# A convolution's kernel table split once and stored in two parts, its Toeplitz rows loaded per part

## What is computed

```python
x = x + _L0_cond_ref(x, log_dt, C, log_A_real, A_imag, D, length)   # a long convolution in time
x = x + einsum('bct,bcd->bdt', x, W1[itok])                         # a 32x32 mix chosen per batch item
x = x + einsum('bct,bcd->bdt', x, W2[itok])                         # another
x = x + lora_mlp(x, W_gate, W_up, W_down, A_*, B_*, itok2)          # gated MLP 512-1376-512 with LoRA
# the convolution:
K = 2.0 * einsum('hn,hnl->hl', Ct, exp(P)).real      # one kernel of 512 taps per channel h
y = causal_convolution(u, K) + u * D[:, None]
return y * (arange(T) < length)                      # masked by each item's length
```

## Time and profile before

| | us |
|---|---|
| three runs | 1174.17, 1175.84, 1176.66; median 1175.84 |
| profiled execution | 1175.31, of which the profile's span is 1173.5 |
| preparation | 0 to 40.3 |
| convolution, to the landing of its last store | 40.3 to 128.8 |
| first inputs of the tiles, until PE works again | 128.8 to 142.3 |
| tile 0 and part of tile 1 | 142.3 to 186.7 |
| steady tiles | 186.7 to 1130.6 |

### The profile page before, as it was taken

The page is one execution under the profiler, slowest core; times in us unless marked ns, Lnnn a source line. Parts: engine busy times, 40 slices in busy tenths (PEclk is TensorE's granted clock), DMA queues, the critical chain, the costliest instruction groups (busy, mean ns, idle before and its releaser), DMA issues.

```text
span 1173.5 us, 19301 instructions
## 1 busy us (share of the span) xinstructions
PE 1062.2 (91%) x6176; PEld 932.3 (79%) x6176; DVE 294.4 (25%) x550; ACT 441.4 (38%) x691; POOL 526.4 (45%) x334
## 2 busy tenths in 40 slices
PE   3577369999999999999999999999999999999998
PEld 3576258888887878888888888787878888888886
DVE  7566212221221222121211222221212221212221
ACT  7543234243333334343424333333433333433331
POOL 0587364343434444443534443444445353544431
PEclk9799679999999999999999999999999999999999
DMA  8688323333324233332333333323333233333321
GB/s 327 221 288 281 121 82 99 102 112 91 108 72 123 69 110 105 98 111 81 109 106 107 89 108 93 114 64 113 93 105 110 81 112 97 107 94 115 96 68 36
DMA packets 100922, 135.52 MB, mean 115 GB/s; under 512 B 26340, under 2 KB 59365, under 8 KB 100901
## 3 DMA queue, kind: packets, MB, share of 16 engines
q1 hardware_dynamic: 99380, 133.35, 37.4%
q10 hardware_dynamic: 1520, 1.92, 0.6%
HBM read 118.21 MB, written 16.99 MB: 115 GB/s over the span
## 4 chain that ended last, share of the span: by engine, by line
SPq 35%; PE 22%; issue 12%; POOL 11%; DMA 11%; ACT 7%; DVE 3%; ACTq 0%; DVEq 0%; POOLq 0%
SPq L339 14%; DMA braw<-in_tb 10%; POOL bst L443 9%; PE ps L979 8%; SPq L188 7%; PE ps L948 6%; ACT bst L572 5%; PE ps L1021 5%; SPq L267 4%; SPq L347 3%; SPq L322 2%; SPq L329 2%; PE ps L969 1%; PE ps L1010 1%; SPq L315 1%
## 5 line engine op out<-in xcount | busy, mean ns | idle before, releaser
L443 POOL TENSOR_TENSOR bst<-braw,bst 128x1024 fp32r<-128x1024 f32 (+1 forms) x96 | 212.2, 2211 | 246.7 <-ACT bst L572 246.7
L979 PE MATMUL ps<-wg_hi,x_hi 128*128 128x512 f32 (+2 forms) x768 | 298.0, 388 | 1.7 <-DVE x_lo L832 1.7
L979 PE MATMUL ps<-wg_hi,x_lo 128*128 128x512 f32 (+2 forms) x768 | 292.1, 380 | 0.0
L979 PE MATMUL ps<-wg_lo,x_hi 128*128 128x512 f32 (+2 forms) x768 | 291.9, 380 | 0.0
L424 POOL TENSOR_TENSOR x_raw<-x_raw,xb 128x512 f32<-128x512 f32 x32 | 41.2, 1286 | 322.2 <-DMA xb<-in_x 322.2
L572 ACT ACTIVATE bst<-braw,odd 128x1024 fp32r<-128x1024 f32 (+1 forms) x96 | 103.6, 1079 | 184.8 <-DMA braw<-in_tb 184.1
L979 PEld LDWEIGHTS ps<-wg_hi,x_lo 128*128 128x128 f32 x768 | 145.2, 189 | 25.7
L979 PEld LDWEIGHTS ps<-wg_hi,x_hi 128*128 128x128 f32 x768 | 145.8, 190 | 22.9 <-issue 2.0
L979 PEld LDWEIGHTS ps<-wg_lo,x_hi 128*128 128x128 f32 x768 | 145.8, 190 | 20.6
L1021 PE MATMUL ps<-wd_hi,at_hi 128*128 128x288 f32 (+1 forms) x704 | 159.0, 307 | 1.8 <-DVE at_lo L855 1.4
L588 ACT ACTIVATE at_hi<-ps 128x512 fp32r<-128x512 f32 (+1 forms) x96 | 54.0, 562 | 274.0 <-PE ps L1010 273.1
(11 more groups left out here) (142 smaller groups left out, 1309.0 us busy)
## 6 DMA issues: line engine op xcount, KB each, us to landing
braw<-in_tb SPq DMA_DIRECT2D x256, 128.0 KB, 2.7
braw<-in_tb SPq DMA_DIRECT2D x128, 96.0 KB, 2.4
adraw<-in_tad SPq DMA_DIRECT2D x128, 88.0 KB, 2.1
ur<-in_xT SPq DMA_DIRECT2D x16, 512.0 KB, 4.3
x1p<-yo SPq DMA_DIRECT2D x16, 512.0 KB, 3.3
x_raw<-x1p SPq DMA_DIRECT2D x32, 256.0 KB, 2.8
xb<-in_x SPq DMA_DIRECT2D x32, 256.0 KB, 3.0
agraw<-in_ta SPq DMA_DIRECT2D x128, 64.0 KB, 2.3
```

Of the source, the lines that this page charges most:

```text
L443: sub(v, b_from(q), v.bitcast(F32), ALU.subtract).then_inc(s["blo"], 1)
L979: last = mm(bank[:, 0:n], x3s[a][:, k, :], wgs[b][:, k, o:o + n], start=(k == 0 and a + b == 0), stop=False, skip_group_check=True)
```

## The change

The table `kf` is split while it is still 16 x 1024: ACT copies it to `kf_hi`, DVE subtracts to `kf_lo`. Both are stored, to `kpad[0]` and `kpad[1]`, the second after the first. The Toeplitz matrix of a pair is now two DMAs of 512 KB, one from each part, straight into the float32r tile `tp`, which holds three pairs (`NTP = 3`). `ts_hi` and `ts_lo` are gone. SP issues the first three pairs as soon as both parts are in DRAM, then pair q + 3 when PE is done with pair q. The input `ur` keeps its two pairs, the output `yo` too. The loops are written out. The eight `w_low` of POOL now stand at the head of its program.

```diff
-    kpad = nc.dram_tensor("kpad", (C, P + T), F32, kind="Internal").ap()
+    kpad = nc.dram_tensor("kpad", (2, C, P + T), F32, kind="Internal").ap()
...
+        def load_toeplitz(eng, q):
+            for a in range(2):
+                src = kpad[a, 2 * q:2 * q + 2, 0:T]
+                src = bass.AP(src.tensor, src.offset, [[1, P], [P + T, 2], [1, T]])
+                eng.dma_start(tp[:, q % NTP, a].bitcast(F32), src).then_inc(s[f"tt{q % NTP}"], 16)
+
+        def load_u(eng, q):
+            p = q % 2
+            eng.dma_start(ur[:, 2 * p:2 * p + 2, :], xT[2 * q:2 * q + 2].rearrange("c p w -> p c w")
+                          ).then_inc(s[f"u{p}"], 16)
...
+            sp.wait_ge(s["kout"], 64)
+            for q in range(NTP):
+                load_toeplitz(sp, q)
+
+            for q in range(C // 2):
+                if q + 2 < C // 2:
+                    sp.wait_ge(s["usp"], 2 * q + 2)
+                    load_u(sp, q + 2)
+                if q + NTP < C // 2:
+                    sp.wait_ge(s["y"], 2 * q + 2)
+                    load_toeplitz(sp, q + NTP)
+                sp.wait_ge(s["ev"], 2 * q + 2)
+                sp.dma_start(x1p_bct[:, 2 * q:2 * q + 2, :], yo[:, q % 2]).then_inc(s[f"yst{q % 2}"], 16)
...
-            def lows(it):
-                for k in range(4):
-                    pool.wait_ge(s["thi"], it * 4 + k + 1)
-                    nc.gpsimd.tensor_tensor(ts_[1][:, k, :], tr[:, k, :], ts_[0][:, k, :].bitcast(F32),
-                                            ALU.subtract).then_inc(s[f"tsp{k}"], 1)
-
-            for it in range(C // 4):
-                lows(it)
-                if it < 6:
-                    w_low(it)
-            for k in range(4):
-                pool.wait_ge(s[f"tsp{k}"], C // 4)
+            for n in (0, 1, 2, 3, 4, 5, 9, 10):
+                w_low(n)
...
             ag_low(0)
-            w_low(9)
-            w_low(10)
             b_low(0, 0, 0)
...
             act.wait_ge(s["kf"], 1)
-            act.dma_start(kpad[:, P - 1:P - 1 + T].rearrange("h (i j) -> i h j", j=UI), kf[:]).then_inc(s["kout"], 16)
-
-            for k in range(4):
-                act.wait_ge(s[f"u{k // 2}"], 16)
-                nc.scalar.activation(us[0][:, k, :], ur[:, k, :], ACT.Copy).then_inc(s["uhi"], 1)
-            w_high((7,))
-            act.wait_ge(s["kout"], 32)
+            nc.scalar.activation(kfs[0][:], kf[:], ACT.Copy).then_inc(s["khi"], 1)
+            act.wait_ge(s["khi"], 1)
+            act.dma_start(kpad[0, :, P - 1:P - 1 + T].rearrange("h (i j) -> i h j", j=UI), kfs[0][:].bitcast(F32)
+                          ).then_inc(s["kout"], 16)
+            act.wait_ge(s["klo"], 1)
+            act.dma_start(kpad[1, :, P - 1:P - 1 + T].rearrange("h (i j) -> i h j", j=UI), kfs[1][:].bitcast(F32)
+                          ).then_inc(s["kout"], 16)
+            act.wait_ge(s["kout"], 64)
             act.wait_ge(s["tst"], 16)
...
+            def u_high(h):
+                q = h // 2
+                act.wait_ge(s[f"u{q % 2}"], 16 * (q // 2) + 16)
+                if h >= 4:
+                    act.wait_ge(s["y"], h - 3)
+                nc.scalar.activation(us[0][:, h % 4, :], ur[:, h % 4, :], ACT.Copy).then_inc(s["uhi"], 1)
+
+            for h in range(4):
+                u_high(h)
             act.dma_start(w_part(wg_raw, wd_raw, NW - 1), w_hbm(NW - 1)).then_inc(s[f"wl{NW - 1}"], 16)
-
-            w_high(range(8, NW - 1))
-
-            highs(0, True)
+            w_high(range(7, NW - 1))
+            for h in range(4, 8):
+                u_high(h)
             w_high((NW - 1,))
-            with act.Fori(1, C // 4) as it:
+            for h in range(8, C):
+                u_high(h)
+            act.wait_ge(s["y"], C)
...
+            dve.wait_ge(s["khi"], 1)
+            dve.wait_ge(s["kf"], 1)
+            V.tensor_tensor(kfs[1][:], kf[:], kfs[0][:].bitcast(F32), ALU.subtract).then_inc(s["klo"], 1)
+
             w_low(6)
...
+            def out_of_psum(h):
+                q = h // 2
+                dve.wait_ge(s["y"], h + 1)
+                if q >= 2:
+                    dve.wait_ge(s[f"yst{q % 2}"], 16 * (q // 2))
+                V.tensor_tensor(yo[:, q % 2, h % 2, :], yp[h % 4], mk[:], ALU.mult).then_inc(s["ev"], 1)
+
+            for h in range(4):
+                u_low(h)
+            w_low(7)
+            w_low(8)
+            for h in range(C):
+                out_of_psum(h)
+                if h + 4 < C:
+                    u_low(h + 4)
...
+            for h in range(C):
+                q = h // 2
+                pe.wait_ge(s["usp"], h + 1)
+                pe.wait_ge(s[f"tt{q % NTP}"], 32 * (q // NTP) + 32)
+                if h >= 4:
+                    pe.wait_ge(s["ev"], h - 3)
...
-            pe.wait_ge(s["wlo"], 6)
+            pe.wait_ge(s["wlo"], 8)
```

More of the change, by code:

```diff
@@ L59 @@
 K_PN = 568
+NTP = 3
 UCOLS, VCOLS = C * UN, C * UI
@@ L126, in cond_resid_kernel @@
         zer = sb("zer", [C, P])
-        kf = sb("kf", [UN, C, UI])
+        kf_hi = sb("kf_hi", [UN, C, UI], F32R)
+        with ExitStack() as raw_only:
+            kf = sbin(raw_only)("kf", [UN, C, UI])
+        kfs = [kf_hi, sb("kf_lo", [UN, C, UI], F32R)]
         wms = sb("wms", [C, NCOND, 2, C])
@@ L133, in cond_resid_kernel @@
         us = [sb("us_hi", [P, 4, KT * B], F32R), sb("us_lo", [P, 4, KT * B], F32R)]
-        ts_ = [sb("ts_hi", [P, 4, T], F32R), sb("ts_lo", [P, 4, T], F32R)]
-        yo = sb("yo", [P, 4, T])
-        tr = sb("tr", [P, 4, T])
+        tp = sb("tp", [P, NTP, 2, 2, T], F32R)
+        yo = sb("yo", [P, 2, 2, T])
         ur = sb("ur", [P, 4, KT * B])
@@ L161, in cond_resid_kernel @@
         outb = sb("outb", [P, T])
-        names = """pk cst cstp small lens w12 zer kf kout wm wms tst u0 u1 tt0 tt1
-            a1 da dch ph tg kuv kps uhi thi usp0 usp1 usp2 usp3 tsp0 tsp1 tsp2 tsp3 whi wlo wlv y0 y1 y2 y3
-            ev0 ev1 ev2 ev3 yst0 yst1 done wz msk
+        names = """pk cst cstp small lens w12 zer kf kout wm wms tst u0 u1 tt0 tt1 tt2
+            a1 da dch ph tg kuv kps uhi usp khi klo whi wlo wlv y
+            ev yst0 yst1 done wz msk
             xin xsum x1hi x1lo wbd x3mm x3n x3t x3hi x3lo
@@ L249, in _ @@
             sp.dma_start(ixs[:], idx).then_inc(s["small"], 16)
-            for p in range(2):
-                sp.dma_start(ur[:, 2 * p:2 * p + 2, :], xT[2 * p:2 * p + 2].rearrange("c p w -> p c w")
-                             ).then_inc(s[f"u{p}"], 16)
+            for q in range(2):
+                load_u(sp, q)
             for n in range(NW - 1):
@@ L487, in _ @@
             act.wait_ge(s["zer"], 1)
-            act.dma_start(kpad[:, 0:P - 1], zer[:, 0:P - 1]).then_inc(s["kout"], 16)
+            for a in range(2):
+                act.dma_start(kpad[a, :, 0:P - 1], zer[:, 0:P - 1]).then_inc(s["kout"], 16)
             act.wait_ge(s["da"], 1)
@@ L518, in _ @@
-            act.dma_start(w_part(wg_raw, wd_raw, NW - 1), w_hbm(NW - 1)).then_inc(s[f"wl{NW - 1}"], 16)
-            w_high(range(8, NW - 1))
[L522 to L529, removed]
@@ L780, in _ @@
             V.tensor_tensor(d0, d0, dsk[:], ALU.add).then_inc(s["kf"], 1)
+            dve.wait_ge(s["khi"], 1)
+            dve.wait_ge(s["kf"], 1)
+            V.tensor_tensor(kfs[1][:], kf[:], kfs[0][:].bitcast(F32), ALU.subtract).then_inc(s["klo"], 1)
             w_low(6)
[L784 to L817, removed]
+            def u_low(h):
+                dve.wait_ge(s["uhi"], h + 1)
+                V.tensor_tensor(us[1][:, h % 4, :], ur[:, h % 4, :], us[0][:, h % 4, :].bitcast(F32),
+                                ALU.subtract).then_inc(s["usp"], 1)
+            def out_of_psum(h):
[4 more added lines that the diff above has]
+                V.tensor_tensor(yo[:, q % 2, h % 2, :], yp[h % 4], mk[:], ALU.mult).then_inc(s["ev"], 1)
@@ L938, in _ @@
             PASSES = ((0, 0), (0, 1), (1, 0))
-            def conv_block(it, first):
-                for k in range(4):
-                    pe.wait_ge(s[f"usp{k}"], it + 1)
-                    pe.wait_ge(s[f"tsp{k}"], it + 1)
-                    if not first:
-                        pe.wait_ge(s[f"ev{k}"], it)
-                    for c in range(KT):
-                        for a, b in PASSES:
-                            last = mm(yp[k][:, c * P:T], us[a][:, k, c * P:(c + 1) * P], ts_[b][:, k, 0:T - c * P],
-                                      start=(c == 0 and a + b == 0), stop=(c == KT - 1 and a == 1))
-                    last.then_inc(s[f"y{k}"], 1)
-            conv_block(0, True)
-            with pe.Fori(1, C // 4) as it:
-                conv_block(it, False)
+            for h in range(C):
[4 more added lines that the diff above has]
+                    pe.wait_ge(s["ev"], h - 3)
+                for c in range(KT):
+                    for a, b in PASSES:
+                        last = mm(yp[h % 4][:, c * P:T], us[a][:, h % 4, c * P:(c + 1) * P],
```

(3 more changed lines are left out.)

11 lines of the change are left out of this document (2 added, 9 removed).

## The result

| | before | after |
|---|---|---|
| median (range), us | 1175.26 (1174.17 to 1176.66) | 1211.43 (1210.75 to 1214.1) |
| profiled execution, span | 1173.5 | 1210.2 |
| `kf` complete; its store (before) or its copy to `kf_hi` (after) starts | 29.7 | 46.9 |
| first Toeplitz issue | 32.68 | 52.58 |
| last store of the convolution landed | 128.77 | 169.20 |

The ratio is 1.0305, interval [1.0283, 1.0327]: the change makes the kernel slower by 36.2 us. The forecast was 1205.2 with a range of 1185 to 1220. The span grew by 36.7: 17.2 before `kf`, 2.7 for the split, 20.5 in the convolution, -3.7 behind it.

The account below looks back on a forecast made before the run. The convolution was taken as bound by loads, partly their bytes and partly the round trip from freed slot to next landing. Terms 18.7 + 2.6 + 15.3 - 7.2 = +29.4 us gave 1205.2 us, range 1185 to 1220.

Parts of the forecast that it names:

- The forecast's case: All four terms together, +29.4 us, giving a median of 1205.2 us; chance 0.55.
- Part 1: Preparation: six POOL weight subtractions each cost DVE's chain to kf one POOL instruction, +18.7 us; bounds 0, 6.2 and 18.8.
- The rival in which DVE keeps its turn: Preparation: only two of the six subtractions hold DVE up, 12.5 us less, 1192.7 us; chance 0.14.
- Part 2: Between kf and the second store: an ACT copy and a DVE subtraction with two hand-offs, +2.6 us.
- Part 3: Convolution, first Toeplitz issue to last store's landing: 111.4 us against 96.1, +15.3; bounds +9.2 and +20.5.
- so I take the middle, 6.7 us a pair: Convolution: pace chosen between the DMA bytes' 6.23 and the ur loop's 7.1 us a pair.
- its 7.1: Convolution: loop of ur landing (median 4.3), us_hi, us_lo, evacuation, hand-offs and store issue, 7.1 us a pair.
- Two of the signs named for this part: Convolution: ur issues 6.2 to 7.1 us apart, and DMA share above 0.9.
- The other floor: Convolution: DMA time for two Toeplitz loads, one ur and one store, 6.23 us a pair against PE's 3.95.
- The price of 1.77: Convolution: DMA time of one 512 KB Toeplitz load, 1.77 us of all 16 engines, against 1.42 for an ur.
- The rival of cheap Toeplitz rows: Convolution: Toeplitz rows cost no more than ur rows once the queue never runs dry, 11.2 us less, 1194.0; chance 0.08.
- Part 4: Tile 0: without w_low(9) and w_low(10), b_low starts 6.3 us earlier and PE need not restart at 1.2 GHz, -7.2 us.

Follow-up runs that it names:

- alone in the kernel before: Kernel before, with POOL's w_low(0) to w_low(5) moved to the head of its program: 1191.51 us, ratio 1.013.
- alone in the gap: Kernel before, with only w_low(9) and w_low(10) moved from tile 0 to between the convolution's end and the first tile's inputs: 1168.07 us, ratio 0.9939.
- changed order: Changed kernel, with DVE evacuating both heads of a pair before the two us_lo of two pairs on: 1193.47 us, ratio 1.0151.
- POOL held back: Changed kernel, with POOL starting its weight subtractions only when DVE has made kf_lo: 1202.82 us, ratio 1.0235.
- one Toeplitz load, old order: Changed kernel, loading only the high part of the Toeplitz rows, one 512 KB load a pair instead of two: 1204.54 us, ratio 1.025.
- rows 256 bytes apart: Changed kernel with both evacuations before the us_lo, Toeplitz row starts 256 bytes apart instead of 4, both loads reading one part of kpad: 1186.9 us.
- the same row: Changed kernel with both evacuations before the us_lo, Toeplitz loads reading one row, starting on 256 bytes, for all 128 partitions: 1196.47 us.
- 260 bytes apart: Changed kernel with both evacuations before the us_lo, Toeplitz row starts 260 bytes apart, both loads reading one part of kpad: 1189.32 us.
- the same row, 4 bytes on: Changed kernel with both evacuations before the us_lo, one Toeplitz row for all 128 partitions, starting 4 bytes off 256 bytes: 1196.25 us.
- paced: Changed kernel, with both evacuations before the us_lo and POOL's eight subtractions let go one a pair after six us_lo: 1177.89 us, ratio 1.0018.
- moved into the convolution: Kernel before, with only w_low(9) and w_low(10) moved from tile 0 into the fifth and sixth round of the convolution: 1174.66 us, ratio 0.9985.

## Why the prediction was right, point by point

The time lay inside the range, 6.2 above the forecast. The forecast's case came true and not a rival; its terms, measured in the profiled executions:

| term | predicted | measured | shown by |
|---|---|---|---|
| 1. POOL against DVE's chain | +18.7 | +17.2 | trace; alone in the kernel before, +17.1 to the store of `kf` |
| 2. the split | +2.6 | +2.7 | trace |
| 3. the convolution | +15.3 | +20.5 | trace; order, bytes and both apart |
| 4. tile 0 | -7.2 | -3.7 | trace; alone in the gap, -6.9 behind the convolution |

**Part 1** was right in mechanism and count: six turns. The price was taken as the whole POOL instruction, 3.13; DVE's own instruction runs inside what is left, so the excess was about 2.8. The rival in which DVE keeps its turn fell: DVE's rows at 23.40 to 35.58 follow each other without a gap, and each waits once. The rule of the Trainium skill (SBUF — State Buffer, "SBUF: two separate sides") that the loser waits out the whole instruction agrees with the rows of 3.00 to 3.14 us. That L727 and L728, with one tensor input of 32 elements, wait too agrees with the same page ("Who interferes with whom"), which lets `tensor_scalar` enter the modes that take the pair.

**Part 2** held: 46.90 to 52.58 is 5.7 against 3.0.

**Part 3** had the two floors and went wrong in the choice between them; the weak step is "so I take the middle, 6.7 us a pair". The loop ran at 7.27, above its 7.1. The reason given for the middle, that the median landing of 4.3 holds waits behind other transfers, took off what was not there to take: the loop's landings were 4.87 on the mean, and with a quarter of the traffic gone still 4.53, with the pair at 6.93. The bytes came in only through these 0.34 us. The floor by bytes, 5.77 when the queue is full, lay below and was no reason to go down from the loop's number. In numbers: the first stretch was 1.3 shorter than predicted (14.0 to the landing of the third `ur`), the 13 pairs took 93.8 instead of 87.1, the end 8.8 instead of 8.95. Two of the signs named for this part did not come: the pairs lie outside 6.2 to 7.1, and the DMA share stayed under 0.9.

That 7.1 itself came so near is partly luck: the landings were 0.57 longer than the median it took, the steps between them 2.40 instead of 2.8. And that the stage's +20.5 is the very number of the upper bound is chance: longer pairs and a shorter start cancel.

The other floor was over-read for a full queue: predicted 6.23 a pair, measured 5.77. The price of 1.77 for a Toeplitz load was no misreading of its window, though. It comes back in the stage after the change: 0.89 x 7.27 less 0.67 x 6.93, with and without the load (shares of the windows of 80 to 110 us), is 1.83 us of all 16 engines, an estimate. In the changed order the same difference is 1.04 x 5.77 less 0.98 x 4.67, or 1.42, and the pair itself is 1.10 shorter, which is a lower bound if the loop holds part of the 4.67. So the busy time that a load takes was no fixed price here; in the fuller queue it was smaller. The rival of cheap Toeplitz rows was right that they cost less than 1.77 once the queue is full; that they cost no more than `ur` rows is not shown. It had little effect, because the bytes do not set this kernel's pace: half of the Toeplitz loads left out gave 6.9 us, not the 25 to 29 of a kernel that waits for bytes.

The rule of the Trainium skill named there (DMA: Bandwidth & Descriptors, "How a descriptor splits into AXI transactions") is not shown to be the reason. By that rule the 71 beats are the charge for some starts only; over starts 4 bytes apart it is 65 to 72 and 68 on the mean. An estimate by it for rows moved off 256 bytes is 32 x 1.42 x 4.4 / 64, or 3 us. The runs with spread rows are 2.4 us apart in the median with intervals wider than that, and their pairs take 5.30 off 256 bytes and 5.35 on it: they can neither confirm nor exclude it, but most of the 6.6 us must come from something else. The two kernels with one row for all do not test it, since it charges a start 4 bytes on only one beat more.

**Part 4** was right in its mechanism and too high by 3.5 in the profiled execution. `b_low` started when predicted. Two later landings took part of it: `xb` landed after 3.05 instead of 2.73, `agraw` after 3.85 instead of 2.20. And PE idled 2.2 us instead of 8, but its clock fell all the same: it started again at 2.4 GHz (a matmul of 512 columns took 0.39 at 202.56), and from 203.06 on each took 0.63. Two windows (PE's busy time first, its granted clock third from the end):

```profile
199.50:202.00 2.50, 0.30 (x3) 0.06 (x1) 0.52 (x1) 1.80 (x3) 2.50 (x3) 1.00 0.11 20
202.00:207.00 5.00, 5.00 (x17) 4.01 (x18) 0.56 (x1) 1.96 (x3) 0.27 (x2) 0.66 0.34 100
```

The twelve matmuls took 4.34 against 4.69 before, so most of the 1.9 for the clock did not come. But how much of this is the kernel and how much the one execution? The rest of the span was 1044.7 and 1045.6 in the two kernels with `w_low(9)` and `w_low(10)` in tile 0. In the kernels that have them elsewhere it was:

| kernel | rest, us |
|---|---|
| after | 1041.0 |
| POOL held back | 1039.0 |
| DVE's order | 1038.2 |
| one Toeplitz load, old order / changed order | 1039.3 / 1040.6 |
| rows 256 bytes apart / the same row | 1037.4 / 1039.6 |
| 260 bytes apart / the same row, 4 bytes on | 1038.8 / 1040.0 |
| paced | 1037.7 |
| before, moved into the convolution / into the gap | 1039.2 / 1037.8 |

The gain is 3.7 to 7.3 us against 1044.7, with a mean near 6; after's own execution has the least of it. The estimate of 7.2 was at the upper edge, and some 2 of the 3.5 that the table misses belong to after's one execution.

The two errors, 5.2 too little in part 3 and 3.5 too much in part 4, point the same way, and 1.5 too much in part 1 against them; that the whole came within 6.2 owes a little to this.

## What to carry to other kernels

Moving idle-looking POOL work forward is not free when it reads SBUF beside a DVE chain on the critical path: count one POOL instruction for each DVE instruction it meets, and put it where DVE waits for something else anyway (the gap at 128.8 us was worth 7 us, the same two instructions in the convolution nothing). In a loop with few buffers write out what each engine does in order before costing its transfers: one subtraction standing in front of an evacuation cost 18 us, where leaving out a whole 512 KB load a pair gave 6.9. Take the mean of a landing for such a loop, not the median: a few long ones are part of every turn's cost. And where a round trip and the bytes give two floors near each other, forecast the higher one, not the middle; here the higher one was still 0.17 us a pair too low.

## What was not expected of the hardware

- With both engines asking, DVE and POOL took strict turns: five POOL subtractions of 3.05 us in a row let through one DVE instruction each, which then lasted 3.0 to 4.0; so did two that alone take 0.2 and have one tensor input.
- A 512 KB landing in a loop of round trips kept its median of 4.4 us when the DMA share went from 0.89 to 0.67; its mean went from 4.87 to 4.53 (7.27 and 6.93 us a pair). In a full queue the same load took 7.3 to 8.5, while throughput rose from 284 to 376 GB/s.
- The busy time of the DMA engines that one more 512 KB load a pair adds was 1.83 us in the loop and 1.42 in the full queue (estimates from the shares of the windows of 80 to 110 us).
- 128 rows of 2 KB within 2.5 KB cost a load some 0.2 us against the same rows spread; their start on or off 256 bytes cost nothing that these runs resolve (medians 2.4 us apart, inside the intervals).
- After 2.2 us of idling in tile 0 PE started again at 2.4 GHz, and its clock fell within about 1 us: the granted clock was 0.66 on the mean of the next 5 us (twelve matmuls 4.34 us, against 2.75 a little later).
